# An attention layer and a block-sparse feed-forward layer interleaved by step in one program block

## What is computed

```python
x = x + _L0_xattn_ref(_layernorm(x), ctx_4096, ctx_4096, Wq, Wk, Wv, Wo)   # 32 heads of 16, 8 key heads
x = x + _L0_ffn_ref(_layernorm(x), c1_w, c2_w, w1, w2t)

# _L0_ffn_ref: 512 -> 1792 hidden units in blocks of 32, rank 16
inter = xf @ c1_w.T @ c2_w.T
idx = jnp.argmax(blk, axis=-1) + jnp.arange(0, INTER, SPARSITY)   # one winner in each block
h = jax.nn.relu(jnp.einsum('bkm,bm->bk', w1[idx], xf))
out = jnp.einsum('bk,bkm->bm', h, w2t[idx])
```

## Time and profile before

| what | value |
|---|---|
| median of three runs | 1517.04 us |
| the profiled execution, its span | 1517.68 us, 1516.0 us |
| TensorE matmuls busy | 1394.9 us (92%) |
| VectorE busy | 1078.9 us (71%) |
| ScalarE busy | 763.0 us (50%) |
| GpSimd busy | 719.9 us (47%) |
| HBM read | 53.27 MB |

### The profile page before, as it was taken

How to read it: one execution, slowest core, us unless ns; L and a number is a source line. 1 busy time by engine, 2 the same in 40 slices (tenths; PEclk the granted TensorE clock), 3 DMA queues, 4 the chain that set the end, 5 groups by cost and what they waited for, 6 DMA issues and landing times. The chain is left out here.

```text
span 1516.0 us, 31472 instructions
## 1 busy us (share of the span) xinstructions
PE 1394.9 (92%) x11336; PEld 833.2 (55%) x11352; DVE 1078.9 (71%) x2125; ACT 763.0 (50%) x2476; POOL 719.9 (47%) x748
## 2 busy tenths in 40 slices
PE   5898699998999999887999999999999788889998
PEld 4685344445777777434555555555555235434444
DVE  7998555645766766667989888898877779965212
ACT  5777363223434433337766666666665457655111
POOL 4787452002443434845666566665665306734000
PEclk9999699999999999999999999999999899989999
DMA  7999582126999989656876655645544401546000
GB/s 192 184 173 168 129 179 45 32 39 129 188 169 199 170 141 138 125 139 150 154 146 112 116 117 111 140 106 114 105 81 77 123 3 35 124 84 112 19 10 28
DMA packets 524571, 174.63 MB, mean 115 GB/s; under 512 B 482577, under 2 KB 507601, under 8 KB 524417
## 3 DMA queue, kind: packets, MB, share of 16 engines
q1 hardware_dynamic: 524416, 172.62, 59.4%
HBM read 53.27 MB, written 2.10 MB: 37 GB/s over the span
## 5 line engine op out<-in xcount | busy, mean ns | idle before, releaser
L1946 POOL TENSOR_TENSOR a_q_ss<-a_q_ss,half 128x4 f32<-128x4 f32 x64 | 90.2, 1409 | 167.6 <-DVE a_q_ss L1855 83.9
L1768 ACT ACTIVATE a_probs<-a_masked,a_negmax 128x128 f32<-128x128 f32 x256 | 99.6, 391 | 101.5 <-DVE a_negmax L1826 101.5
L67 PE MATMUL bank<-a_wq_hi,xn_pair 128*128 128x512 f16 (+1 forms) x384 | 140.1, 365 | 6.6 <-DVE a_kn L1860 5.2
L1285 POOL TENSOR_TENSOR a_p_hl<-a_probs,a_p_hl 128x512 f16<-128x512 f32 x64 | 74.4, 1164 | 142.0 <-DVE a_p_hl L1209 142.0
L68 PE MATMUL bank<-a_wq_lo,xn_pair 128*128 128x512 f16 (+1 forms) x384 | 139.9, 364 | 0.0
L69 PE MATMUL bank<-a_wq_hi,xn_pair 128*128 128x512 f16 (+1 forms) x384 | 139.8, 364 | 0.0
L67 PE MATMUL bank<-a_wo_hi,a_o_hi 128*128 128x512 f16 x256 | 97.8, 382 | 4.4 <-DVE x_state L1842 3.5
L68 PE MATMUL bank<-a_wo_lo,a_o_hi 128*128 128x512 f16 x256 | 97.6, 381 | 0.0
L69 PE MATMUL bank<-a_wo_hi,a_o_lo 128*128 128x512 f16 x256 | 97.5, 381 | 0.0
L1961 POOL TENSOR_TENSOR a_normal<-a_probs,a_recip 128x512 f32<-128x512 f32 x64 | 90.2, 1410 | 5.0
L716 POOL TENSOR_TENSOR a_p_hl<-a_probs,a_p_hl 128x512 f16<-128x512 f32 x64 | 77.7, 1224 | 23.8 <-DVE a_p_hl L627 17.1
(11 more groups left out here) (467 smaller groups left out, 5028.4 us busy)
## 6 DMA issues: line engine op xcount, KB each, us to landing
a_no<-in_L_xattn_Wo SPq DMA_DIRECT2D x9, 1024.0 KB, 5.7
a_nq<-in_L_xattn_Wq SPq DMA_DIRECT2D x8, 1024.0 KB, 5.7
a_n_wq<-in_L_xattn_Wq SPq DMA_DIRECT2D x4, 768.0 KB, 5.1
a_n_wo<-in_L_xattn_Wo SPq DMA_DIRECT2D x4, 768.0 KB, 5.3
a_nk<-in_L_xattn_Wk SPq DMA_DIRECT2D x9, 256.0 KB, 3.1
a_nv<-in_L_xattn_Wv SPq DMA_DIRECT2D x9, 256.0 KB, 3.1
f_v_hat<-in_L_ffn_w SPq DMA_DIRECT2D x2, 1152.0 KB, 6.2
x_state<-in_x SPq DMA_DIRECT2D x8, 256.0 KB, 5.0
```

The source lines that it names most:

```text
L67: pe.matmul(out, lh, rh, start=start, stop=False)
L1285: pool.tensor_tensor(p_hl[s % PN][:, 1, t, :], probs[unit(s, t) % PROBS][:, :, :].rearrange("p h n -> p (h n)"), p_hl[s % PN][:, 0, t, :], ...
L1768: m = act.activation(probs[s % 2][:, h, :], src, ACT.Exp, bias=negmax[s % 2][:, h:h + 1], accum_out=total[s % 2][:, h:h + 1])
L1946: pool.tensor_tensor(r[:, :], r[:, :], K.half[:, 0:n], ALU.pow).then_inc(root_done.sem, 1)
```

## The change

The two layers become two sets of generators (`Stage`), and one program block takes a step of the attention, then a step of the sparse layer shifted by 73, on each engine's stream (`side_by_side`, `in_turn`). The semaphore clearing and the barrier between them go. `Front` goes. All that the sparse layer does ahead of its step 0 is put between the attention's steps 48 to 72:

- Rows 0 to 3: VectorE normalises all four in step 64, TensorE turns them (f32, 4 transposes each, steps 64 and 65) into ring banks; ScalarE copies the high halves from the bank (steps 64, 65), VectorE makes the low halves (steps 65, 66). Before, they were split first and turned by DMA.
- Small weights: loaded in step 50, high halves in 64, low halves in 65, those of c2 in two column groups.
- compress(0..3) in steps 66 to 69, score and choice of part 0 in 67 to 70.
- The first two pieces of w1 and w2 (four loads of 512 KB) are issued in step 66, split in steps 68 (w1/0), 70, 71, 72.
- The projection of batch 6 comes in one go in step 72, of batch 7 in step 75; they are added in steps 73 and 76. Step 75 is step 2 of the sparse layer, so batch 7's projection lies between up(1) with side(0), side(1) and up(2).
- side(0) moves one step, behind up(1).
- Parts (b, 1) are picked in steps 2, 2, 3, 3; (b, 2) in steps 4 to 7; (b, 3) in steps 7 to 10 as before. In step 7, (0, 3) comes ahead of (3, 2).
- Rows 4 to 7: statistics gathered in step 4, normalised in steps 5 to 8 (before 2 to 5), compressed in 7 to 10 (before 4 to 7). Their picks keep their steps.
- The layers' banks overlap: `down` collects in 2, 3, 4, 6, the ring is 5, 7, 0, 1, and first uses wait for the attention's last use of the bank. Most buffers of the sparse layer are placed over buffers of the attention, with waits for their last use (`place_free`, `weights_split`, `rows_used`, `probs_turned` and others).

```diff
+BESIDE = 73
...
+def in_turn(a, b, shift, program_a, program_b):
+
+    for t in range(min(a.first, b.first + shift), max(a.end, b.end + shift)):
+        if a.first <= t < a.end:
+            next(program_a)
+        if b.first <= t - shift < b.end:
+            next(program_b)
+    for program in (program_a, program_b):
+        for _ in program:
+            pass
...
-    LOAD_SMALL, MEAN_FRONT, CLEAR_FRONT, HIGH_FRONT, LOW_FRONT, LOAD_FIRST = TOTAL - 14, TOTAL + 1, TOTAL + 2, TOTAL + 3, TOTAL + 10, TOTAL + 14
-    AHEAD = {B: TOTAL + 2, B + 1: TOTAL + 3, B + 2: TOTAL + 11, B + 3: TOTAL + 12}
+    OUT_LATE, ADD_LATE = {B - 2: TOTAL + 8, B - 1: TOTAL + 11}, {B - 2: TOTAL + 9, B - 1: TOTAL + 12}
...
+    beside = lambda t: t - BESIDE
+    FIRST, LAG, RING, MASKS = beside(48), 2, 2, 4
+    LOAD_SMALL, LOAD_FIRST = beside(50), beside(66)
+    CLEAR_SMALL, SMALL_HIGH, SMALL_LOW = beside(52), beside(64), beside(65)
+    MEANS, ROOTS, CLEAR, CONSTANTS, LATER = beside(61), beside(62), beside(65), beside(69), 4
+    NORMAL = beside(64)
+    TURN = {0: beside(64), 1: beside(64), 2: beside(65), 3: beside(65)}
+    ROWS = {b: b + 1 for b in range(HALF, B)}
+    CX = {b: beside(66) + b if b < HALF else ROWS[b] + 2 for b in range(B)}
+    EARLY_PICK = {(b, 0): beside(67) + b for b in range(HALF)}
+    EARLY_PICK.update({(b, 1): 2 + b // 2 for b in range(HALF)})
+    EARLY_PICK.update({(b, 2): 4 + b for b in range(HALF)})
+    EARLY_PICK.update({(b, 3): 7 + b for b in range(HALF)})
+    PICK = {(b, i): EARLY_PICK[b, i] if b < HALF else 4 * (i + 1) + b for b in range(B) for i in range(PARTS)}
...
+    Y_BANKS, RING_BANKS = (2, 3, 4, 6), (5, 7, 0, 1)
+    SPLIT = {("w1", 0): beside(68), ("w1", 1): -3, ("w2", 0): -2, ("w2", 1): -1}
...
+    side_at = lambda t: {0: [], 1: [0, 1]}.get(t, live(t))
...
+        def ring_free(use):
+            if ring.nth[use] == 0:
+                over.bank_over(pe, RING_BANKS[ring.slot[use]])
+            pe.wait_ge(ring.freed(use), ring.n_free(use))
...
+        def turn(b):
+            use = ("turn", b)
+            pe.wait_ge(normal_done.sem, normal_done.count(b))
+            ring_free(use)
+            for k in range(KT):
+                m = pe.transpose(ring[use][:, k * P:(k + 1) * P], xn[b][:, k * P:(k + 1) * P], K.ident[:, :])
+            m.then_inc(ring.filled(use), 1)
...
+            for b in at(TURN, t):
+                turn(b)
+            for u in live(t):
+                up(u)
+            for u in side_at(t):
+                first_of_block(u)
+            for part in at(PICK, t):
+                score(part)
+            for b in at(CX, t):
+                compress(b)
+            for u in live(t - LAG):
+                down(u)
+            yield
...
-        K.end_stage()
-        blocks_ffn(K, front, early)
-        K.in_use.append(front.first_in)
+        blocks = blocks_ffn(K, c, attention, *(a[f"L0_ffn_{w}"] for w in ("c1_w", "c2_w", "w1", "w2t")), early)
+        side_by_side(K.nc, attention, blocks, BESIDE)
```

More of the change, by code:

```diff
@@ L171, in low @@
                               self.K.xn_hi[:, :, b * P:(b + 1) * P], ALU.subtract).then_inc(self.ring.freed(b), 1)
[L174 to L200, removed]
@@ new lines, in first_attention, with weights_split, rows_used @@
+    stage = Stage(FIRST, END, sync, tensor, scalar, vector, gpsimd)
+    stage.place, stage.taken = place, taken
+    last, final = B - 1, TOTAL - 1
+    def weights_split(engine):
+        engine.wait_ge(wlo_done.sem, len(pieces))
+    def rows_used(engine):
+        engine.wait_ge(clo_done.sem, clo_done.count(last))
+        engine.wait_ge(xlo_done.sem, xlo_done.count(last))
+        for b in (last - 1, last):
+            landed(engine, xt_in, b)
+        engine.wait_ge(q_bank.filled(last), q_bank.n_filled(last))
@@ new lines, in blocks_ffn @@
+    at = lambda table, t: [use for use, when in table.items() if when == t]
+    steps = range(FIRST, TILES + LAG + 1)
+    ring_uses = [use for t in steps
+                 for use in ([("turn", b) for b in at(TURN, t)] + [("up", u) for u in live(t)]
+                             + [("side", u) for u in side_at(t)] + [("s", part) for part in at(PICK, t)]
+                             + [("cx", b) for b in at(CX, t)])]
+    y_bank = Banks(K, f"{N}_y", [K.bank[i] for i in Y_BANKS], [(hf, n) for hf in range(2) for n in range(HALF)])
@@ new lines, in blocks_ffn @@
+    ring = Banks(K, f"{N}_ring", [K.bank[i] for i in RING_BANKS], ring_uses)
+    w_here = {k: [sem(f"{k}_in{i}") for i in range(RING)] for k in nat}
+    pieces = sorted(SPLIT, key=SPLIT.get)
+    whi_done, wlo_done = Steps(sem("whi"), pieces), Steps(sem("wlo"), pieces)
+    mean_done, root_done, const_done, zeroed, small_in = (sem(n) for n in ("mean", "root", "const", "zeroed", "small_in"))
+    small_hi, small_lo = Steps(sem("small_hi"), ["c1", "c2"]), Steps(sem("small_lo"), ["c1", "span", "rest"])
@@ new lines, in turned, with width, chosen, mask_landed @@
+    def turned(b):
+        return ring[("turn", b)][:, :].rearrange("p (k t) -> p k t", k=KT)
+    def width(part):
+        return min(SPAN, NT - SPAN * part[1]) * P
+    def chosen(part):
+        m, n = parts.index(part) % MASKS, width(part)
+        blocks = lambda t: t[:, 0:n].rearrange("p (n k) -> p n k", k=BLK)
+        return blocks(mask[m]), blocks(ring[("s", part)]), top[m][:, 0:n // BLK]
+    def mask_landed(engine, part):
+        engine.wait_ge(mask_in[parts.index(part) % MASKS], 16 * (parts.index(part) // MASKS + 1))
```

1691 lines of the change are left out of this document (880 added, 811 removed).

## The result

The changed kernel took 1528.47 us (median of four runs, 1527.17 to 1530.75) beside 1517.13 us for the kernel before on the same chip: a ratio of 1.0078, 95% interval 1.0061 to 1.0096. It is slower by some 12 us, outside the predicted range of 1509.5 to 1522.0.

A forecast was written before the change was run, and what follows sets the result against it. TensorE's matmuls bound the sparse layer's steady part, with some 12 us to win at the seam. Summed: 11.2 - 0.65 - 3.2 - 2.3 - 4.4 = 0.65 us gained, so 1516.4 us; eight in ten: 1509.5 to 1522.

The forecast's parts named there:

- the wait that takes the barrier's place: Batch 7's projection waits for its heads, queued on GpSimd behind weight pieces and turned at 180.4; TensorE idles 2.3 us.
- the adding of batch 7 and its statistics: VectorE work in the sparse layer's step 2, behind two choices: 1.4 us, delaying hidden(3).
- X(3): X(u) is the moment of side(u)'s weight load in the sparse layer; an undisturbed step lasts 5.6 us.
- rival (b): Slower: the clock falls in the new waits, likeliest three restarts costing 5 us, time near 1521; chance 0.27.
- What the prediction took from the same page on transposes: The 16 transposes at 148 to 152 us don't keep the clock up, leaving the projections cold, as batch 6's was priced.
- The seam's chain: Compress, copies, score of batches 0 to 3 follow one another between the attention's last steps; last score at 167.7.
- X(2): Weight load of side(2), after which nothing stalled for long: at 187 against 198.2 before, 11.2 us gained.
- Three more scores: Three more scores than before lie behind X(2) on TensorE: 0.65 us lost.
- side(4): Waits for the mask of part 1 of all four batches, landing at X(3)+9.0: stall 3.2 us, bounds 0 and 5.
- side(8): Waits for the choice (3,2), now in step 7, landed at X(7)+10.2: stall 2.3 us, bounds 0 and 5.
- The ring: Four banks with five uses in steps 7 to 10: compress waits 1.4 each, net 4.4 us lost, bounds 2.8 and 5.6.
- Rival (a): The seam's gain stays, only ring waits and scores are paid: 6 to 8 us faster, near 1510; chance 0.31.

The follow-up runs named there:

- e1: Changed kernel with batch 7's output added into x one step earlier (step 75 instead of 76): 1524.41 us, ratio 1.0054 to the kernel before.
- e2: Changed kernel with choices of part 1 of batches 0 to 3 a step earlier (1, 1, 2, 2): 1527.58 us, ratio 1.0082 to the kernel before.
- e4: Changed kernel with choices of part 2 of batches 0 to 3 back in steps 3 to 6: 1523.86 us, ratio 1.0064 to the kernel before.
- e7: e6 plus the edit of e3: 1512.07 us, ratio 0.9982 to the kernel before.
- e6: e5 plus later batches' rows and compress, and choices of part 2, at the steps of the kernel before: 1512.87 us, ratio 0.9968 to that kernel.
- e8: e7 plus compress groups of batches 0 to 3 in pairs, two in one step: 1509.29 us, ratio 0.9957 to the kernel before.
- e11: e8 with choices of part 1 in steps 1, 2, 2, 2 instead of 1, 1, 2, 2: 1506.49 us, ratio 0.9936 to the kernel before.
- e3: Changed kernel with GpSimd's low part of batch 7's heads ahead of w2 pieces 0 and 1: 1528.26 us, ratio 1.0085 to the kernel before.
- e5: Changed kernel with the edits of e1 and e2 together: 1524.28 us, ratio 1.0051 to the kernel before.
- e9: e6 without the edit of e2, part 1 staying where the change has it: 1520.71 us, ratio 1.0024 to the kernel before.
- e12: e8 with all four choices of part 1 in step 2: 1510.01 us (median of seven runs), ratio 0.9955 to the kernel before.

## Why the prediction was wrong

**The step that failed** is the sentence on the projection of batch 7, "the wait that takes the barrier's place", and its end: "the adding of batch 7 and its statistics (1.4), so hidden(3) starts at X(3)+1.7". I had the addition in VectorE's queue behind two choices and counted only what stands behind it there. I did not ask who waits for it through its bank. The change joins two blocks of code, and bank 6 is the attention's projection bank and one of the sparse layer's four output banks; the barrier had kept that apart. It was the longest wait, 4.27 us, and with its restart 6.0, where the sum has nothing; e1 removes exactly that.

**The second thing that failed** is that the sum prices its new waits without a fall of the clock and leaves that to rival (b). The two came together: the prediction's own sign of being wrong, a clock below 1.00 between 190 and 260 us, is there (0.83 from 190 to 200, 0.87 from 210 to 220, 0.83 from 240 to 250). Behind the waits of 4.27, 2.88 and 2.62 us the matmuls started 0.43 apart, at the lower of the two levels, and cost 1.74 (11.84 less 5.83, less the wait), 1.35 (6.97 against 5.62 in e2) and 1.14 (X(8) to X(9) 9.04 against 7.90). That is 4.2 us in three restarts; the rival said 5 in three. Its 1521 is still 7 us short of the 1528.5 measured, chiefly since it lacks the bank too. The rule cited, of the Trainium skill, TensorE: Matmul & The Clock Gate, section HAM oscillation — how this bites in real kernels, is one that this trace bears out for these three waits; e4's wait of 2.94 us, behind which the clock stayed at 1.00, shows that it doesn't hold for each. The argument against it, that gaps of 1.1 to 1.5 us left the clock at 1.00 in the earlier trace rows, was sound only for gaps of that size: the clock is 1.00 from 230 to 240 and from 250 to 260 us, around waits of 1.23.

**What the prediction took from the same page on transposes** (that they don't count as busy for the clock) is not borne out by this trace. In the changed kernel the matmuls ahead of eight f32 transposes are slow, and the first ones behind them are fast, with only 17-column mixes beside them:

```profile
152.82 0.63 PE L69 MATMUL bank<-a_wo_lo,a_o_t 128*128 128x512 f16 x1
153.24 0.63 PE L70 MATMUL bank<-a_wo_hi,a_o_t 128*128 128x512 f16 x1
153.67 1.52 PE L2348 MATMUL bank<-ident,f_xn 128*128 128x128 f32 x8
...
155.34 0.38 PE L68 MATMUL bank<-a_wo_hi,a_o_t 128*128 128x512 f16 x1
155.55 0.38 PE L69 MATMUL bank<-a_wo_lo,a_o_t 128*128 128x512 f16 x1
```

e7 has the same: 0.43 us apart at 150.84 and 151.27, 0.22 apart from 154.73 on, eight transposes and mixes between. So the clock rose while TensorE did nothing but transposes and mixes; whether it was the transposes that raised it, no run separates. Batch 6's projection did begin slow (168.90 and 169.33), as the sum has it, but behind the waits of the four scores, so the transposes needn't have anything to do with it.

Step by step:
- The seam's chain: scores at 159.5, 161.6, 165.6 and 168.5 against 158.6, 161.3, 165.0 and 167.7. Right within 1 us, although the four normalised rows took 4.4 us where I had under 2.4.
- The heads of batch 7: ended 177.7 on GpSimd (predicted 177.0), projection at 181.94 (180.4), since it was 4.2 us from the turn's issue at 177.74. X(2) at 188.6 instead of 187: 9.6 gained, not 11.2.
- Three more scores: X(2) to X(3) is 5.83 in e1, 0.22 more than before for its one further score: the price was right.
- side(4): X(3) to X(4) 9.06, predicted 9.0. The cause was right, the tenth is luck: with the addition already over, hidden(3) started at X(3)+1.3 instead of +1.7 and the choices ended at +6.4 instead of +6.6, and the last mask took 2.7 us to land instead of 2.4.
- side(8): X(7) to X(8) 10.86, predicted 10.2; wait 2.62 for 2.3.
- The ring: four waits of 1.23, predicted 1.4 each; steps 9 and 10 last 7.90 and 7.89, predicted 7.9. What I took as given, that these compress groups must stand there, cost these 4.9 us of waits: at the steps of before they don't wait at all (e6).
- The sum of what is off: 1.6 (X(2)) and 4.3 (the bank) and 4.2 (clock) and 0.5 (the waits at 200 to 265 us, 10.4 for 9.9), together 10.6 of the 11.0 us between the predicted 0.65 gained and the 10.4 lost at X(27); 0.4 is left in the steps without a wait. From X(27) to the end the profiled execution wins 1.0 of this back (the span is 9.4 longer), within the scatter of 4.9 us that this part has from execution to execution.

Rival (a) needed masks that arrive as just in time as before and no fall of the clock, and had neither. Its 1510 is about what e8 reaches, and e11 lies some 10 us below the kernel before: the idea was worth that much, and the order of the queues gave it away.

## What to carry to other kernels

When a barrier between two stages goes, list for each bank (and buffer) that both use its last reader on one side and first writer on the other, and read the reader's place in its engine's queue: a wait that no one had before begins there. Predicted waits and the clock's fall are one case and not rivals: behind side(4), side(8) and the first 'down', every wait of 2.6 us or more but one brought some 1.1 to 2.7 us of slow matmuls along. The length alone doesn't tell: 2.94 us in e4 brought none, and 2.00 us ahead of the last projection in e11 brought eight matmuls 0.43 apart, 1.7 us. An edit that takes away one wait is worth it only if the next stage's own due date is met too: e2 and e3 won nothing alone that the times can tell, and e2's edit nothing on top of e1's (e5), but on top of e6's early rows the trace has it worth 6.3 us (e9 against e6). For e3's edit no run shows a gain in time, alone or on e6. All that was kept, with the compress groups in pairs and one of e2's early choices, makes e11, 0.5 to 0.8% faster than the kernel before.

## What the runs showed of the hardware that was not expected

VectorE's cast of the same 128x512 tile took 0.42 us at 152.80, with GpSimd idle, and 2.26 at 172.35, in the middle of three GpSimd operations; its four normalised rows took 4.43 us beside GpSimd's 3.75, where one takes 0.54 in e7.

```profile
148.45 4.43 DVE L2511 TENSOR_SCALAR f_xn<-x_state,f_mv,f_rstd 128x512 f32<-128x512 f32 x4 [0.63 <-POOL f_rstd L2626]
152.80 0.42 DVE L627 CAST a_o_hl<-a_o_nat 128x512 f16<-128x512 f32 x1
...
171.90 0.42 DVE L619 TENSOR_TENSOR a_o_nat<-bank,a_recip 128x256 f32<-128x256 f32 x1
172.35 2.26 DVE L627 CAST a_o_hl<-a_o_nat 128x512 f16<-128x512 f32 x1
174.54 0.68 DVE L631 SCALAR_TENSOR_TENSOR x_state<-bank,x_state 128x512 f32<-128x512 f32 x1
```

The operations around it that read a bank (0.42 and 0.68) kept their time beside the same GpSimd work. GpSimd's three started at 170.11 and last 2.17 each, so the second ended near 174.4, just ahead of the cast's end at 174.61. The Trainium skill, SBUF — State Buffer, section Who interferes with whom, says that a cast or a tensor_scalar of VectorE in its fast mode and a GpSimd operation exclude each other for the whole of an instruction; the row agrees, the cast having stood until one GpSimd operation was over; in e3, where it starts at 174.31 behind the end of GpSimd's operation at 174.21, it took 0.43. It cost little here, as GpSimd reached the heads only 1.95 us behind the cast's end, but it is the price that a step moved under GpSimd's work should have carried.

The profiled execution of e12 took 6817 us with TensorE shown busy for 6765.7 of them at a granted clock of 1.00, while VectorE's busy time was the usual 1070.8; its seven other runs lie between 1505.6 and 1515.0. Its 'up' matmuls start 1.28 us apart (699.76, 701.04, 702.32) instead of 0.22. No run here tells why.
